# One product in four of a selective scan goes from VectorE to GpSimd, with a new order of all engines' steps

## Chip, cores and metric

One core of a Trainium2 chip runs the whole program in one launch. The metric is the device time of an execution in microseconds. All data is fp32.

## Reference

The input x is 8 sequences (batches) of 512 tokens of 128 values. Six layers follow each other, each added to its input:

```python
x = x + 0.5 * ffn0(layernorm(x))        # norm, 128->512, gelu, norm, 512->128, ternary weights
x = x + attn0(layernorm(x))             # small scan over the tokens, 16 states
x = x + 0.5 * ffn0(layernorm(x))
x = x + 0.5 * ffn1(layernorm(x))        # encoder, router over 8 experts, top 2, decoder, norm
x = x + attn1(layernorm(x))             # selective scan, below
x = x + 0.5 * ffn1(layernorm(x))
```

attn1 has 256 inner channels d with 16 states n each. After a projection and a convolution over 3 tokens give u and a gate, and a projection of u gives B, C and (with a softplus) delta, it computes in chunks of 32 tokens, each starting from zero:

```python
dA  = exp(delta[l, d] * A[d, n])
dBu = delta[l, d] * B[l, n] * u[l, d]
h   = dA * h + dBu                      # along the tokens of a chunk
y[l, d] = sum over n of h * C[l, n]
out = (y * silu(res)) @ W_out + b_out
```

## The kernel before

A batch is one tile of 512 tokens. Its work is cut into parts, and every engine has four threads of parts: F (the two ffn0 layers and attn0), P (everything that uses the one PSUM bank pp: the router half of ffn1, called front, twice per batch; the part of attn1 ahead of the scan; and the product with W_out behind it), E (the experts and the decoder of ffn1, called back) and S (the selective scan). The parts of pp take turns in a fixed row (P_TURNS), and a turn starts when the one before has left the bank (bank_free). Several batches are under way at once: while one is in its scan, a later one is in ffn0.

Inside an engine the order of all steps is written out by hand: ORDER has one string per engine, one letter per step, and side_by_side takes the next step of the thread that the letter names. An engine issues in that order and waits at a step until its semaphores are there. A further letter K in TensorE's string is a filler: a product of a tile of zeros (256 columns) that adds nothing to yp. There are 44 of them in 33 places.

The scan of a batch has 16 steps (2 channel halves c of 128 by 8 pairs of states k), 128 steps in all, and each step j has two half-steps r, one per state, of 128 x 512 elements:

- SyncE loads the rows of B and C, broadcast to 128 partitions, into b_row and c_row (three slots each; L502, L509). A slot is free when its last reader is done.
- GpSimd makes dbu of a whole step, du times b_row (L708, 128 x 1024); dbu has two buffers, so it waits for the scans of step j - 2. du itself (L635) needs delta, the last output of the part ahead of the scan.
- ScalarE makes dA of a half-step, the exponential (L1207), into one of two PSUM banks. It waits until the product of the half-step before in that bank is done, since that reads the bank.
- VectorE runs the scan in place in that bank (L982) and then the product with C into hs (L989), which has two buffers.
- TensorE adds the product into yp through the identity (L1483), in the order of the steps. At the end of each channel half VectorE multiplies yp with the gate (yg, L997).

TensorE's products take two passes in fp32, so a step of 512 columns is two instructions in the profile. The other lines that matter here: L1228 with pp and yg (the product with W_out), L1151 (delta), L662 and L675 (GpSimd's multiplication by the norm's gain and its addition in the back part), L1300 (a product of attn0), L1492 (the filler).

Of the kernel before, what the change touches and what calls it, by code (L numbers as in the profile page):

```python
# [27 lines left out]
ALU = mybir.AluOpType  # L28
# [33 lines left out]
    "PE":
        "PFEPFEFFFFFFFFFFFFFFFFFFFFFFFFPFPFFPFFPFPEFFPPPKKKKEKFEFEEEFEFEKKFFKFPFPFFFPFFPPPKPFPFKKFFSSKPSFSFPS"
        "FPSFPSSFKPESSSPSKSKSFSFSESEFSEFEESESFSESFFSFSSSSFFFSPFFPSSSPFSPFPFPFPFFPFFFSKKSPSSPSPSPSEPSFSFPSPSSF"
        "SSFESKESEFSFEESSFESSFSESFFSFSFFSSPSPPFSSPFSPFFPFPKFFPFFSSPSSPSSPSPSEPSFSFPSPSPKSSFEPSEPFEPSEPEPESFEF"
        "SEFFSEFSFEFPSEFPEEPESSPSESSPSFSPSSPSKPFSFSFFSKFPSFPSFPSFKPSSFSEPSSSPKKKPSPSFPSFEPSSEPSEFEEPFEPEFFESF"
# [1524 lines left out]
```

## Time and profile before

| | us |
|---|---|
| median of 3 runs | 1121.41 |
| fastest and slowest of them | 1113.58 and 1122.65 |
| span of the profiled execution, first to last instruction | 1116.6 |
| the profiled execution's own time | not listed apart from the runs |
| TensorE busy (modelled ends) | 935.0 |
| VectorE busy | 762.5 |
| ScalarE busy | 659.4 |
| GpSimd busy | 515.7 |
| mean granted clock of TensorE, of full speed | 0.933 |

The profile is one execution. Busy times overlap between engines; the matmuls are pipelined and their ends are modelled, so TensorE's share is no measure of how near it is to its peak. An engine's idle time costs something only where a later step waits for it.

### The profile page before, as it was taken

Reading aid. Unit: us, or ns where it says so; the run is one execution under the profiler, and the core shown is the slowest. Engines: PE = TensorE matmul, PEld = TensorE weight load, DVE = VectorE, ACT = ScalarE, POOL = GpSimd, SP = SyncE. Lnnn points to the kernel's source line nnn. Section 1 sums busy time; section 2 is a strip of 40 time slices with the busy share of each in tenths; the row PEclk is TensorE's granted clock in tenths of the full one; section 3 lists DMA queues with packets and bytes.
Section 4 is the critical chain, followed back from the end, with each engine's and each line's share of the span. In section 5 each row is a group of like instructions: output and inputs, shape, how many; then the busy total and the mean of one; then the engine's idle time right before and its main releaser. Section 6 shows DMA issues by size and latency. Waiting matters only on the chain.

```text
span 1116.6 us, 11275 instructions
## 1 busy us (share of the span) xinstructions
PE 935.0 (84%) x3446; PEld 451.9 (40%) x3446; DVE 762.5 (68%) x1717; ACT 659.4 (59%) x1030; POOL 515.7 (46%) x413
## 2 busy tenths in 40 slices
PE   6457888799889979998999799969996898689865
PEld 4234344344434434444444344434433343343332
DVE  3213417983898388878896699748974959499921
ACT  4344557576657765796668855866585424644221
POOL 2131227462745365556454654555454616555311
PEclk9668999999989989999999999989998899889986
DMA  3002017441735263456252744255434525374320
GB/s 136 10 1 86 1 54 249 143 132 48 246 120 164 73 229 130 167 158 210 86 181 96 227 180 163 92 172 208 142 123 136 202 108 206 119 270 134 142 86 9
DMA packets 44717, 151.83 MB, mean 136 GB/s; under 512 B 4464, under 2 KB 12784, under 8 KB 40560
## 3 DMA queue, kind: packets, MB, share of 16 engines
q1 hardware_dynamic: 44656, 151.11, 39.5%
q8 instruction: 27, 0.44, 0.2%
q14 instruction: 34, 0.28, 0.1%
HBM read 148.21 MB, written 2.88 MB: 135 GB/s over the span
## 4 chain that ended last, share of the span: by engine, by line
PE 46%; DVE 25%; ACT 14%; issue 6%; POOL 6%; DMA 2%; SPq 0%; DVEq 0%; POOLq 0%; ACTq 0%
DVE dA L982 11%; PE yp L1483 9%; ACT L116 5%; PE mp L1442 5%; PE pp L1362 4%; PE mp L1427 3%; PE fp L1264 3%; PE fp L1248 3%; PE pp L1228 3%; DVE hs L989 3%; ACT dA L1207 2%; PE mp L1451 2%; POOL dbu L708 2%; PE mp L1228 2%; PE pp L1332 1%
## 5 line engine op out<-in xcount | busy, mean ns | idle before, releaser
L708 POOL TENSOR_TENSOR dbu<-du,b_row 128x1024 f32<-128x1024 f32 x128 | 301.2, 2356 | 178.8 <-DVE dA L982 176.9
L982 DVE TENSOR_TENSOR_SCAN dA<-dA,dbu 128x512 f32<-128x512 f32 x256 | 312.4, 1220 | 75.5 <-ACT dA L1207 41.5
L1483 PE MATMUL yp<-hs,ident 128*128 128x512 f32 x512 | 273.1, 636 | 58.2 <-DVE hs L989 57.7
L1207 ACT ACTIVATE dA<-delta,pr 128x512 f32<-128x512 f32 x256 | 173.8, 686 | 104.3 <-DVE hs L989 103.1
L989 DVE TENSOR_TENSOR hs<-dA,c_row 128x512 f32<-128x512 f32 x256 | 177.0, 691 | 28.1 <-PE yp L1483 18.2
L116 ACT ACT_TABLE_LOAD x130 | 166.8, 1283 | 15.0 <-POOL delta L639 11.4
L1483 PEld LDWEIGHTS yp<-hs,ident 128*128 128x128 f32 x512 | 89.7, 196 | 169.4 <-DVE hs L989 101.7
L1427 PE MATMUL mp<-cont,ex_ 64*128 64x512 f32 x128 | 75.5, 671 | 15.5 <-DVE he L940 11.6
L1431 PE MATMUL mp<-cont,ex_ 64*128 64x512 f32 x128 | 75.6, 672 | 3.2 <-DVE he L945 3.2
L1248 PE MATMUL fp<-sq,w 128*128 128x512 f32 x128 | 71.1, 679 | 5.7 <-ACT sq L1030 4.1
L1264 PEld LDWEIGHTS fp<-w,hT 128*128 128x128 f32 x512 | 63.5, 193 | 29.2 <-issue 14.1
L1264 PE MATMUL fp<-w,hT 128*128 128x129 f32 x512 | 66.6, 279 | 5.4 <-ACT sq L1030 2.1
L940 DVE SCALAR_TENSOR_TENSOR he<-mp,nb_e,gsp 128x512 f32<-128x512 f32 x64 | 47.5, 742 | 23.7 <-PE mp L1427 15.9
L1442 PE MATMUL mp<-he,ex_ 128*64 128x512 f32 x128 | 63.6, 640 | 0.0
L1444 PE MATMUL mp<-he,ex_ 128*64 128x512 f32 x128 | 63.6, 640 | 0.0
L662 POOL TENSOR_TENSOR dg<-eoT,ex_ 128x512 f32<-128x512 f32 x16 | 17.5, 1092 | 78.6 <-DVE eoT L949 78.6
L805 DVE COPY fs<-fp 128x4 f32<-128x4 f32 x16 | 2.5, 157 | 70.9 <-PE fp L1284 70.9
L1362 PE MATMUL pp<-p_zT,mw_cv 128*128 128x512 f32 x96 | 48.9, 618 | 0.8 <-ACT du L1137 0.8
L1043 ACT ACTIVATE hT<-fp,b 128x512 f32<-128x512 f32 x64 | 42.6, 685 | 11.3 <-PE fp L1248 10.6
L569 POOL TENSOR_SCALAR f_vv<-f_mv 128x4 f32<-128x4 f32 x24 | 4.6, 193 | 94.0 <-DVE f_mv L774 93.5
L945 DVE SCALAR_TENSOR_TENSOR he<-mp,nb_e,gsp 128x512 f32<-128x512 f32 x64 | 47.5, 742 | 0.0
L1178 ACT ACTIVATE eoT<-mp 128x512 f32<-128x512 f32 x16 | 9.5, 596 | 58.3 <-PE mp L1444 58.3
(219 smaller groups left out, 1426.9 us busy)
## 6 DMA issues: line engine op xcount, KB each, us to landing
b_row<-held SPq DMA_DIRECT2D x104, 512.0 KB, 4.9
c_row<-held SPq DMA_DIRECT2D x104, 512.0 KB, 4.1
gsp<-gheld SPq DMA_DIRECT2D x32, 1024.0 KB, 6.6
xin<-L_attn_x SPq DMA_DIRECT2D x8, 256.0 KB, 3.0
out<-xb SPq DMA_DIRECT2D x8, 256.0 KB, 2.3
ex_<-c_ex SPq DMA_DIRECT2D x1, 1001.0 KB, 8.0
b_row<-c_ps SPq DMA_DIRECT2D x1, 768.0 KB, 9.4
pr<-c_pr SPq DMA_DIRECT2D x1, 567.0 KB, 10.4
```

Source lines behind the costliest of these rows:

```text
L116: self.act.preload_act_table_set(sets[0])
L708: pool.tensor_tensor(out=dbu[:, j % 2, :].rearrange("p (r t) -> p r t", r=2), in0=d, in1=b_n, op=ALU.mult).then_inc(dbu_r.sem, 1)
L982: dve.tensor_tensor_scan(out=dA[:, half], data0=dA[:, half], data1=dbu[:, j % 2, half], initial=0.0, op0=ALU.mult, op1=ALU.add).then_inc(h ...
L989: dve.tensor_tensor(out=hs[:, j % 2, half], in0=dA[:, half], in1=c_row[:, C_ROWS.slot[j], half], op=ALU.mult).then_inc(hc_r.sem, 1)
L1207: act.activation(out=dA[:, r * SEQ:(r + 1) * SEQ], in_=delta[:, i % 2, c, :], func=ACT.Exp, scale=mA[:, c, 2 * k + r:2 * k + r + 1]).then_ ...
L1248: pe.matmul(fps[(c + 1) % 2], lhsT=w1[:, c * P:(c + 1) * P], rhs=fzT, start=True, stop=True).then_inc(h_ps.sem, 1)
L1264: pe.matmul(o[:, q, 0:P + 1], lhsT=hT[:, c, q * P:(q + 1) * P], rhs=w2[:, c, 0:P + 1], start=(c == 0), stop=(c == HC - 1))
L1362: last = pe.matmul(pp[:, :], lhsT=mw_cv[:, k, c * P:(c + 1) * P], rhs=pzT[:, k:k + SEQ], start=(k == 0), stop=(k == TAPS - 1))
L1427: pe.matmul(mps[0], lhsT=w_e1[0:MOE, k, :], rhs=cont[0:MOE, m % 2, :], start=True, stop=True).then_inc(hee_ps.sem, 1)
L1431: pe.matmul(mps[1], lhsT=w_e1[MOE:2 * MOE, k, :], rhs=cont[MOE:2 * MOE, m % 2, :], start=True, stop=True).then_inc(heo_ps.sem, 1)
L1442: last_e = pe.matmul(mps[0][0:MOE, :], lhsT=w_e2[:, 2 * k, :], rhs=he[:, 2 * k, :], start=False, stop=(k == EP - 1))
L1483: pe.matmul(yp[:, :], lhsT=ident[:, :], rhs=hs[:, j % 2, r * SEQ:(r + 1) * SEQ], start=(s % PAIRS == 0 and r == 0), stop=(s % PAIRS == PAI ...
```

## The change

Of the 128 scan steps, those with j % 4 == 1 (32 steps, 64 half-steps, four steps per batch) get their product with C on GpSimd. For them VectorE's scan writes its result into hs in SBUF instead of into the PSUM bank, after it has waited for the sum that last read this buffer; GpSimd multiplies hs in place by c_row, in a new thread C; TensorE's sum and SyncE's next load of that slot wait for GpSimd's semaphore instead of VectorE's; ScalarE's next exponential in the bank waits for the scan only. The other 96 steps work as before. All five order strings are new: GpSimd's has 64 letters C more, TensorE's no K; the counts of all other letters are the same. The fillers, their tile of zeros and its memset are gone. ScalarE loads its table before it waits for the start of a scan instead of after, and GpSimd's product L662 waits for its own addition of the back part before.

```diff
-    "Pool":
-        "PFEFFFFFFFFFPFPFPFFFEEFEPPFFPSSPFSPSSSSFSFSFSSFSFSSEESEPPSFFFPSSPSPFSSFSFSSSSFSSSFEESESPFFSPFSPSSFPSP"
...
+    "Pool":
+        "FPFFFEFFFFFFPFFFFFPPFEEEPPFFFPPSSSCSCFSSFSCCSSFSFFSSCECSPEEPSSFSCCPFFPPSSSCCFSSFPSSCCSSFFSEESCEPFSCS"
...
-FILL = 256
...
+POOL_STEPS = 4
+
+
+def on_pool(j):
+    return j % POOL_STEPS == 1
+
+
+class Products:
+
+
+    def __init__(self, by_vector, by_pool):
+        self.by_vector, self.by_pool = by_vector, by_pool
+
+    def wait(self, eng, h):
+        j, r = divmod(h, 2)
+        some = sum(on_pool(x) == on_pool(j) for x in range(j))
+        eng.wait_ge(self.by_pool if on_pool(j) else self.by_vector, 2 * some + r + 1)
...
-        zeros = sb("zeros", [P, P])
...
-        hc_r = signal("hc_r", STEPS)
+        hc_v, hc_p = sem("hc_v"), sem("hc_p")
+        products = Products(hc_v, hc_p)
...
                             if C_ROWS.after[j] >= 0:
-                                sp.wait_ge(hc_r.sem, 2 * (C_ROWS.after[j] + 1))
+                                products.wait(sp, 2 * C_ROWS.after[j] + 1)
...
                 pool.wait_ge(ddr.sem, ddr.at(m, 1))
+                if m >= 1:
+                    stage, i = M_TURNS[m - 1]
+                    added = hx_new if stage == "moef" else xo_new
+                    pool.wait_ge(added.sem, added.at(i, 1))
...
+            def c_thread():
+                for j in range(BATCH * STEPS):
+                    if not on_pool(j):
+                        continue
+                    for r in range(2):
+                        half = slice(r * SEQ, (r + 1) * SEQ)
+                        yield True
+                        pool.wait_ge(hs_r.sem, 2 * j + r + 1)
+                        if r == 0:
+                            pool.wait_ge(c_in[C_ROWS.slot[j]], 16 * C_ROWS.load[j])
+                        pool.tensor_tensor(out=hs[:, j % 2, half], in0=hs[:, j % 2, half],
+                                           in1=c_row[:, C_ROWS.slot[j], half], op=ALU.mult).then_inc(hc_p, 1)
...
+                            if on_pool(j):
+                                if j >= 2:
+                                    dve.wait_ge(sum_ps.sem, h - 3)
+                                dve.tensor_tensor_scan(out=hs[:, j % 2, half], data0=dA[:, half],
+                                                       data1=dbu[:, j % 2, half], initial=0.0, op0=ALU.mult,
+                                                       op1=ALU.add).then_inc(hs_r.sem, 1)
+                                continue
...
+                            table(ACT.Exp)
                             if h % (2 * STEPS) == 0:
                                 act.wait_ge(start_r.sem, start_r.at(i, 1))
-                            table(ACT.Exp)
-                            if h >= 2:
-                                act.wait_ge(hc_r.sem, h - 1)
+                            if h >= 2 and on_pool(j - 1):
+                                act.wait_ge(hs_r.sem, h - 1)
+                            elif h >= 2:
+                                products.wait(act, h - 2)
...
-                            pe.wait_ge(hc_r.sem, 2 * j + r + 1)
+                            products.wait(pe, 2 * j + r)
...
-            def k_thread():
...
-            side_by_side(ORDER["PE"], F=f_thread(), P=p_thread(), E=e_thread(), S=s_thread(), K=k_thread())
+            side_by_side(ORDER["PE"], F=f_thread(), P=p_thread(), E=e_thread(), S=s_thread())
```

Counted letter by letter, the steps shift against each other. On TensorE, the last matmul of the part ahead of the scan of batch i stands behind this many of the 32 half-steps of the scan before it, for i = 1 to 7: before 31, 31, 30, 31, 32, 32, 32; in the change 31, 27, 27, 26, 28, 26, 26. The product with W_out of batch i = 0 to 6 stands behind this many half-steps of the next scan: before 10, 15, 16, 15, 14, 16, 10; in the change 7, 9, 10, 10, 10, 11, 10. In GpSimd's list the C steps of step j mostly stand behind the dbu of step j + 1, in some places behind that of step j + 2 too. ScalarE's table changes, counted along its list, are 130 before and 127 in the change.

## Rows read from the trace of the kernel before

**Rows 1.** The page: busy time and share by engine; VectorE in 40 slices.

```profile
PE 935.0 (84%) x3446; PEld 451.9 (40%) x3446; DVE 762.5 (68%) x1717; ACT 659.4 (59%) x1030; POOL 515.7 (46%) x413
...
DVE  3213417983898388878896699748974959499921
```

**Rows 2.** The page: the chain that ended last, by engine.

```profile
PE 46%; DVE 25%; ACT 14%; issue 6%; POOL 6%; DMA 2%; SPq 0%; DVEq 0%; POOLq 0%; ACTq 0%
```

**Rows 3.** Windows: length, busy PE, PEld, DVE, ACT, POOL, clock, DMA share, GB/s.

```profile
180.00:200.00 20.00, 18.93 (x83) 9.79 (x82) 19.03 (x43) 11.19 (x18) 10.68 (x7) 1.00 0.50 170
...
720.00:740.00 20.00, 15.45 (x70) 8.26 (x69) 8.35 (x28) 11.78 (x18) 6.01 (x7) 0.96 0.32 83
...
1040.00:1060.00 20.00, 17.43 (x55) 6.89 (x55) 18.58 (x29) 3.05 (x5) 5.67 (x3) 1.00 0.27 109
```

**Rows 4.** Groups by line: count, busy us, mean ns, idle before, releasers.

```profile
L982 DVE TENSOR_TENSOR_SCAN dA<-dA,dbu 128x512 f32<-128x512 f32 x256 | 312.4, 1220 | 75.5 <-ACT dA L1207 41.5 <-POOL dbu L708 33.4
...
L708 POOL TENSOR_TENSOR dbu<-du,b_row 128x1024 f32<-128x1024 f32 x128 | 301.2, 2356 | 178.8 <-DVE dA L982 176.9 <-DMA b_row<-held 1.9
...
L989 DVE TENSOR_TENSOR hs<-dA,c_row 128x512 f32<-128x512 f32 x256 | 177.0, 691 | 28.1 <-PE yp L1483 18.2 <-issue 1.3
...
L1492 PE MATMUL yp<-w,zeros 128*128 128x256 f32 x88 | 30.4, 456 | 5.0 <-DVE m_top L924 5.0
...
L662 POOL TENSOR_TENSOR dg<-eoT,ex_ 128x512 f32<-128x512 f32 x16 | 17.5, 1092 | 78.6 <-DVE eoT L949 78.6
...
L675 POOL TENSOR_TENSOR hx<-xf,dg 128x512 f32<-128x512 f32 x8 | 10.1, 1267 | 5.5 <-ACT dg L1025 5.5
```

**Rows 5.** The same windows, products of line 989 alone: length, VectorE, clock.

```profile
180.00:200.00 20.00, 5.53 (x8) 1.00 0.50 170
...
1040.00:1060.00 20.00, 4.15 (x6) 1.00 0.27 109
...
sum 900.00, DVE 176.99; mean DVE 3.93
```

**Rows 6.** Timeline, joints between scans: start, length, engine, line, idle before.

```profile
282.70 1.23 DVE L982 TENSOR_TENSOR_SCAN dA<-dA,dbu 128x512 f32<-128x512 f32 x1 [0.68 <-POOL dbu L708]
...
387.39 2.35 POOL L635 TENSOR_TENSOR du<-delta,du 128x1024 f32<-128x1024 f32 x1 [18.27 <-ACT delta L1151]
...
392.41 1.23 DVE L982 TENSOR_TENSOR_SCAN dA<-dA,dbu 128x512 f32<-128x512 f32 x1 [0.89 <-POOL dbu L708]
...
497.68 1.22 DVE L982 TENSOR_TENSOR_SCAN dA<-dA,dbu 128x512 f32<-128x512 f32 x1
...
503.77 1.23 DVE L982 TENSOR_TENSOR_SCAN dA<-dA,dbu 128x512 f32<-128x512 f32 x1 [1.37 <-POOL dbu L708]
```

**Rows 7.** Timeline, the middle of the scan of batch 3.

```profile
545.41 1.22 DVE L982 TENSOR_TENSOR_SCAN dA<-dA,dbu 128x512 f32<-128x512 f32 x1
...
560.03 1.95 PE L1228 MATMUL pp<-pr,yg 128*128 128x128 f32 x16
...
563.34 1.23 DVE L982 TENSOR_TENSOR_SCAN dA<-dA,dbu 128x512 f32<-128x512 f32 x1
```

**Rows 8.** Waits: who waited for whom; total us, times, longest.

```profile
PEld yp L1483 <- DVE hs L989: 101.7, 88, 8.6
...
DVE dA L982 <- POOL dbu L708: 33.4, 10, 10.9
```

**Rows 9.** The chain at 106.90 us, then the timeline of line 1300.

```profile
106.90 3.59 PE yp L1492 x8
...
40.85 2.07 PE L1300 MATMUL fp<-sq,at 128*128 128x512 f32 x2 [0.69 <-ACT sq L1030]
...
540.58 1.02 PE L1300 MATMUL fp<-sq,at 128*128 128x512 f32 x2
```

**Rows 10.** Windows at 40 and 620 us, columns as in rows 3.

```profile
40.00:60.00 20.00, 8.05 (x25) 4.52 (x24) 4.45 (x15) 8.64 (x13) 2.82 (x4) 0.59 0.00 0
620.00:640.00 20.00, 16.28 (x50) 8.19 (x51) 12.21 (x13) 18.55 (x26) 14.15 (x10) 0.91 0.69 231
```

More of the change, by code:

```diff
@@ L47 @@
+        "FSSFSCFPCPPSSSPCCSPFSFSPSCFCSFSEFESESPCSCPFSSSCFCSPPFSEESCCSPPFSSFFSSPCESCFSSEEEPCSSSCFFSFSCCSPPPSFS"
+        "PSCCSEEPFSPFSEFSCCSFSSEEEFSPSCCFSSSPCFSCPPSESEFPSECPSCFSFFPSCSCSFFSEEESPCSSCPSSFSCCSPPSSCPSCSPESESCC"
+        "ESPSSSEEESPCCSSPSSSCCPPSSSCCSEESSSCCSSPESSCCPSSEEPSSECSCPEPEEEEE",
     "DVE":
-        "FEFFPEFFFFFFFFFFPPPFFPFEEEEEEEEFFFEPFFFPSSSSSSSSSSSPPFSFSFSSSEESSEESEFEESFEFSSSSSESSSPSSSFSFFPSSFSSS"
-        "SSFSFSSSPPSSSPSSFSEEFSEEFEESSESSESSSSESSSPSFSFFPSSSSSFSSSSSSFSFSSPPPSSSSEESEEFEESEFPPEFSPSSESEESPEES"
@@ L62 @@
[L62 to L70 removed]
+        "FFFPFFEFFFFFFFFPEPFPFFPEEEEFEEFEFEEPFFFPFSSSSSSSPPFSFSSSSSEESEEEEEESFSFFSSSSSSESSSPSSFSSFPFSSSSSSSSS"
@@ new lines @@
+        "FSSPPFSFSSSSSEESEEEESESEFSFFSSESPSPSSSSFSFSPSFSSSSSSSSSSSPPPSFSFSFSSEPEPSEESEEFPESSFEFSSSESSESPESSSS"
+        "FSEEFFSPEEESSSSSESSSESSSSSPPPFSSFFSSEESSEEPEEPESSEFSFSFSSESPSESPESSSSSFESEFSSFEESESSESPSSESSSSSPPPSF"
+        "SFSFSEESPPEESESEFSEEFFSSSSPESSSEPESEESSSFSEESSFSESEFSSSPSSESSSSPPPSSSFSSFEEFSEEPPEEESSFSEFSFSSESPSSP"
+        "EESESSSSSESEESFSSESESSFPSSSSSSSEPPPSSSSSSSEESEEPEEPEESSSSPESSSSPEEPSSSSEESSESEESESSSSSSSSSSSESSPPSSS"
+        "SSSSEEEESEESEESSSPSSPSSESSSSSPPSSSSSSEEPPEEEEEEPPEEEEEEEEEE",
@@ new lines @@
+    "PE":
+        "PFFFFFFFFFFFFFFEFFFFFFFFFFFPFPFPFFPFEFPFPFFEPPFFEFEFEEEFEFEFFFFPFFFPPPFPFPFPFPFPFFFFPPSSPPSPSPSESSSS"
+        "FFSSSEFESEESFESSEFESFSFSSFSFFSSFFFPSSSPSSPSPSPSPFPFPSFFPFPFFPSFFPSPESSSSPSPSSFSFSESESEFSEEFSESEFFFFF"
+        "FSSSFPFFSPSSPSPSPSSPFPSFPSSFFSSPFFPSFPPFPFESSPSSSPPSPSPFPSFSPEFEPESFSEESEFSEFSFSSFEFFFSSEFFPSPSPSSEP"
+        "SEPESPSSPESPSESFSSEFPFPFPSPFFFPFFPSESSPPSPSSPFSEFPSESFESPEPFESSESESSFSFEFFFSFSFESPFPFPSPSSSEPSSPESFP"
+        "EPESESSSSFEPFPFSPFFFPPSSFFPSSSEPPSPPFEPSSFPSESPFSEFEESESSSFEFSFEFSFSFEFEPFPFSSPSSSPSESPEPESSPSPEFSES"
+        "SPFSPFFPPSPSFFPFEFFSSPSPSSPSPEPFEFSEPESFFEPESSEFSFSFSFSFEFFSEPFPSSPFPSSESPSSPSESPEPSESSESPSSPEPPSPSS"
+        "PSESSPSPSPSPEPSSEEPEEPSESSESSSESEPSPSSPESSSPEPSEPEPSPESSSSSSEPSPSPSPSPPSSSSSSPESSESESSESEEESSEPPSSPS"
+        "PSSPSSPESSSSSSSPEEPPEPEPEPEPEEEEEEEEE",
@@ L557, in _ @@
             ch.add(pool.memset(by32[:, :], 1.0 / 32))
-            ch.add(pool.memset(zeros[:, :], 0.0))
             ch.add(pool.memset(pzT[:, 0:TAPS - 1], 0.0))
@@ L989, in s_thread @@
                             dve.tensor_tensor(out=hs[:, j % 2, half], in0=dA[:, half],
-                                              in1=c_row[:, C_ROWS.slot[j], half], op=ALU.mult).then_inc(hc_r.sem, 1)
+                                              in1=c_row[:, C_ROWS.slot[j], half], op=ALU.mult).then_inc(hc_v, 1)
                         if s % PAIRS == PAIRS - 1:
@@ L1485, in s_thread @@
                                       ).then_inc(sum_ps.sem, 1)
-            def k_thread():
-                order = ORDER["PE"]
-                for at in (n for n, name in enumerate(order) if name == "K"):
-                    yield True
-                    alone = order[:at].count("S") in (0, 2 * BATCH * STEPS)
-                    pe.matmul(yp[:, 0:FILL], lhsT=zeros[:, :], rhs=w1[:, 0:FILL], start=alone, stop=alone,
-                              skip_group_check=True)
-            side_by_side(ORDER["PE"], F=f_thread(), P=p_thread(), E=e_thread(), S=s_thread(), K=k_thread())
+            side_by_side(ORDER["PE"], F=f_thread(), P=p_thread(), E=e_thread(), S=s_thread())
 def stacked(*parts):
```

33 lines of the change are left out of this document (11 added, 22 removed).

## The prediction

> **What bounds the kernel now.** I read five views in this order. First the page's busy times and slices [rows 1]: no engine is full over the span (TensorE 84%, VectorE 68%), but VectorE's row swings between 9 and 1. That is the thing to see: it is full in some stretches and starved in others, so its mean says little. Second, the chain that ended last [rows 2]: it passes from engine to engine, 46% of the span on TensorE, 25% on VectorE, 6% on GpSimd. Third, windows of 20 us over the stretch with scans, 160 to 1060 us [rows 3]: in 21 of 45 windows VectorE is busy 17.5 us or more (first and last shown, with 720 as one of the others: 8.35). So VectorE ends the wait in about half of the stretch only.
>
> Fourth, the joints between two scans [rows 6]. Before batch 2, du waited 18.27 us for delta, that is for the before-scan part, and the first scan follows at 392.41. From the last scan of batch 2 to the first of batch 3 it takes 6.1 us (497.68 to 503.77). Fifth, the middle of a scan [rows 7]: from 545.41 to 563.34 no scan starts, since yg (L997) stands behind the product with W_out of the batch before (560.03) which has its turn in bank pp only then. These two waits come from the serial turns of pp, not from VectorE's load.
>
> **The base of the sum.** The profiled execution has a span of 1116.6 us; its own time is not listed apart. The median of the three runs, 1121.41, lies 4.8 above that span, the fastest run 3.0 below. I sum against the span and add 4.8 at the end. About 1% (11 us) is what a measurement of this kernel can tell from no change.
>
> **VectorE's products.** 32 of 128 steps give up two products of 0.691 us [rows 4]: 64 x 0.691 = 44.2 us of busy time. On the path they lie only where VectorE is full. The 21 full windows hold 91.2 of the 177.0 us of products (in [rows 5] the first, the last and the sum), 51.5%, so 0.515 x 44.2 = **-22.8 us** (bounds 0 and -44.2). The other half falls where VectorE waits anyway. No row has a scan into SBUF. The nearest are the scan into PSUM, 1.220 us, and the product, which reads PSUM, writes SBUF and goes faster [rows 4]; I keep 1.22, and a tenth of a microsecond each way on 64 scans would be 6 us. ScalarE may start the next exponential after the scan instead of after the product, 0.69 us earlier, but VectorE's next scan is all that this feeds, so it is in the 22.8 already.
>
> **GpSimd's products.** Half of L708's 2.356 us is 1.18; other 128x512 products take 1.092 (L662) to 1.267 (L675) [rows 4]. I take 1.18, nearest in its operands: 64 x 1.18 = 75.5 us of GpSimd's time (70 to 81), from 515.7 to 591 us of busy time. It isn't full after that, so what counts is who stands behind. On GpSimd the next dbu does: for step j+2 it may start only when scan j is done, and the second product now comes first. 1.18 + 2.36 = 3.54 us, and VectorE reaches scan j+2 after two scans and two products, 2 x 1.22 + 2 x 0.69 = 3.8 us. The cover is 0.3 us, gone whenever one of GpSimd's other products (1.09 to 1.27 us) slips between. All 32 exposed would be 32 x 1.18 = 38 us. Until now scans waited for dbu 10 times in 128, 33.4 us in sum [rows 8], while dbu waited 176.9 us for scans [rows 4]; I take about a fifth, **+8**.
>
> On TensorE every later instruction stands behind the sum of a GpSimd step. With GpSimd free, the second product is ready 1.18 - 0.69 = 0.49 us later than from VectorE, 16 us over 32 steps; with one dbu queued ahead it is 2.36 + 0.49 = 2.85, 91 us. TensorE's weight loads already wait for a product 88 times, 101.7 us in sum, at 256 sums [rows 8]; the new list puts the sums of these steps further back, and the chain is on TensorE for less than half of its length: **+3**, ends -10 (other matmuls go first) and +42 (0.46 x 91).
>
> The rows of C for these steps come free later, and so do all loads queued behind them on SyncE. With three slots a row is asked for some three steps ahead, 3 x 3.8 = 11 us; a product that is late by 2.85 us eats a quarter of that. Nothing added; without that cover the price is that of the slow rival below.
>
> The Trainium skill, in "GPSIMD Engine Reference", 4.1 Engine selection, speaks against the move: for elementwise work it says VectorE and not GpSimd, about twice as slow with two inputs (3.1: 1.96 times). By that page a product would be an estimated 1.96 x 0.691 = 1.35 us; the halved row of this trace gives 1.7 times. By the page the two GpSimd terms would grow by some 2 us.
>
> **Filler products.** 44 of them (88 passes, 30.4 us busy [rows 4]) in 33 places go. Most are in places where TensorE waits; one group of 3.59 us stands on the chain at 106.90 us [rows 9], so -4. Against it: the granted clock. At 180 to 200 us, with TensorE busy 18.93 us of 20, it is 1.00 [rows 3]; at 40 to 60 us, busy 8.05, it is 0.59 [rows 10], a mix of the levels 2.4 and 1.2 GHz. At the lower one the pair of passes L1300 takes 2.07 instead of 1.02 us [rows 9]. Where the fillers stood, some stretches will now be granted at half. I take +5, net **+1**; ends -30 and +27 (rival below).
>
> **The new order.** Counted letter by letter, the before-scan part of batch i (i = 1 to 7) is moved forward on TensorE: its last matmul stood behind 30 to 32 of the 32 half-steps of the scan before it; now behind 26 to 28, but for batch 1 (31 as before). The product with W_out of batch i comes 7 to 11 half-steps into the next scan instead of 10 to 16. Both aim at the waits in [rows 6, 7]. If every joint fell to the 6.1 us of the best, the seven (23.6, 21.4, 6.1, 7.9, 19.8, 17.3 and 12.8, all read like the third) would give back 66 us. But the period doesn't follow the joint: the batch that ends in the joint of 6.1 us takes 111.4 us from first scan to first scan (392.41 to 503.77), the one that ends in 21.4 takes 109.7 (282.70 to 392.41) [rows 6]. A short joint was paid by a longer scan. I take **-9**, ends -66 and +10 (what is moved forward holds up other work: half of one stall like [rows 7]). ScalarE's table loads fall from 130 to 127 by the letters, and one moves ahead of the wait for start_r, where the first dbu (2.36 us) covers it: both zero. The wait before dg is for an addition that GpSimd issued long before; the memset of zeros is at the start: zero.
>
> **Sum.** -22.8 + 8 + 3 + 1 - 9 = -19.8; 1116.6 - 19.8 + 4.8 = 1101.6 us.
>
> **Rivals.** *The bank pp sets the period.* Its turns (two routers, one before-scan, one product with W_out per batch) form a serial row, and [rows 7] shows VectorE's work waiting for it. For: joints and middles stall at VectorE idle. Then the relief stays only in the first and the last scan, which have no such neighbours in full: about 2 x 8 halves x 0.69 = 11 us, eaten by 8 + 3: 1121.
>
> *TensorE stuck behind GpSimd.* The sums come in order of step, and GpSimd has the dbu of a later step in front of the product in several places of its list. Price 2.85 us per step, 32 steps, times 0.46 of the chain: +42. Then 1121.4 - 22.8 + 42 + 8 + 1 - 9 = 1141. It decides from the point where some 17 of the 32 steps have a whole dbu ahead (17 x 2.85 x 0.46 = 22.3, which eats the gain). Against it: GpSimd idled 178.8 us before L708 [rows 4].
>
> *The clock.* Each of the 33 places loses what 620 to 640 us lost (0.91 instead of 1.00 over 20 us [rows 10], so 1.8 us of work): 59 us, times 0.46: +27 instead of +5: 1124. The Trainium skill, "TensorE: Matmul & The Clock Gate", Why this matters for your kernels, asks to leave no idle gaps between bursts, or the clock falls back. The trace agrees at 40 to 60 us; by that rule the change would end here.
>
> *The joints close.* If two thirds of the 66 us come back: 1101.6 + 9 - 44 = 1067. *The change isn't what it says:* the lists hold 64 letters C and no K, so I give it no chance.
>
> **How the numbers follow.** Forecast 0.48 (its own range 1084 to 1110), joints close 0.10, pp sets the period 0.16, clock 0.09, stuck behind GpSimd 0.17. Faster by over 1%: 0.48 + 0.10 = 0.58; within 1%: 0.25; slower: 0.17. The range 1072 to 1136 leaves out most of the closing joints and the worse half of the slow rival, under 2 in 10.
>
> **What would show it.** VectorE's busy time near 718 us with 192 products; GpSimd near 591; scans into hs still 1.22 us; GpSimd's product 1.09 to 1.27. Right: fewer windows with VectorE over 17.5 us, scans waiting for dbu under some 45 us. Wrong: TensorE's waits before the sums naming GpSimd's product with more than 40 us; the mean granted clock well under the 0.933 of the span now; or joints under 8 us throughout, with a time near 1070.

## The result, and the profile after

The changed kernel takes 1062.81 us (median of 4 runs, 1058.22 to 1066.8) against 1121.22: a ratio of 0.9489 [0.9442, 0.9535], 58 us less. Forecast were 1101.6 us, 20 less, with a range down to 1072. So the side was right, and the forecast size less than half of what came: the time lies at the rival "the joints close" (1067). The profiled execution took 1066.8 us at a span of 1064.9; its mean granted clock is 0.932 (0.933 before).

From the page of the changed kernel: busy time by engine, VectorE's slices, the chain by engine, and the groups that answer to [rows 1, 2, 4].

```profile
PE 918.2 (86%) x3358; PEld 436.9 (41%) x3358; DVE 732.6 (69%) x1653; ACT 651.6 (61%) x1027; POOL 593.8 (56%) x476
...
DVE  3223322996298839885988789777978988699731
...
PE 58%; DVE 17%; ACT 14%; issue 6%; POOL 5%; DMA 0%; DVEq 0%; SPq 0%; POOLq 0%; ACTq 0%
...
L730 POOL TENSOR_TENSOR dbu<-du,b_row 128x1024 f32<-128x1024 f32 x128 | 301.4, 2359 | 112.1 <-DVE dA L1024 90.7
...
L1024 DVE TENSOR_TENSOR_SCAN dA<-dA,dbu 128x512 f32<-128x512 f32 x192 | 234.1, 1219 | 58.3 <-ACT dA L1251 48.9
...
L1031 DVE TENSOR_TENSOR hs<-dA,c_row 128x512 f32<-128x512 f32 x192 | 132.7, 691 | 17.0 <-PE yp L1527 10.4
L743 POOL TENSOR_TENSOR hs<-hs,c_row 128x512 f32<-128x512 f32 x64 | 80.8, 1271 | 41.0 <-DVE hs L1020 40.7
...
L1020 DVE TENSOR_TENSOR_SCAN hs<-dA,dbu 128x512 f32<-128x512 f32 x64 | 76.0, 1209 | 5.4 <-ACT dA L1251 4.7
```

The prices came as forecast: GpSimd's product 1.271 us (taken at 1.18, bounds 1.09 to 1.27), the scan into SBUF 1.209 (taken at 1.22), GpSimd 593.8 us busy (591). VectorE is busy 732.6 us, where 718 were forecast; the last experiments show what the other 14 are. What wasn't forecast is the chain: 12 points have moved onto TensorE, and VectorE's share fell from 25% to 17%. Between the first and the last scan VectorE's row had six slices of 3, 4 or 5 [rows 1]; now there are three of 5 or less, a 2, a 3 and a 5, at the first three joints.

The waits of the changed kernel (total us, times, longest), beside [rows 8]:

```profile
POOL du L653 <- ACT delta L1193: 43.1, 8, 16.4
...
PEld yp L1527 <- DVE hs L1031: 28.8, 34, 3.7
...
PEld yp L1527 <- POOL hs L743: 9.3, 12, 2.0
...
DVE dA L1024 <- POOL dbu L730: 8.9, 3, 5.5
```

TensorE's weight loads wait 28.8 + 9.3 us for products where they waited 101.7; scans wait for dbu 8.9 us where it was 33.4. So neither of the two costs that the prediction put on GpSimd's products shows as a growing wait. Three joints of the changed kernel, on VectorE's timeline (start, length, engine, line, idle before), beside [rows 6]: the last scan of a batch and the first of the next.

```profile
272.88 1.23 DVE L1024 TENSOR_TENSOR_SCAN dA<-dA,dbu 128x512 f32<-128x512 f32 x1 [6.71 <-ACT dA L1251]
...
284.89 1.23 DVE L1024 TENSOR_TENSOR_SCAN dA<-dA,dbu 128x512 f32<-128x512 f32 x1 [5.47 <-POOL dbu L730]
...
387.43 1.23 DVE L1024 TENSOR_TENSOR_SCAN dA<-dA,dbu 128x512 f32<-128x512 f32 x1 [8.13 <-ACT dA L1251]
...
395.06 1.22 DVE L1024 TENSOR_TENSOR_SCAN dA<-dA,dbu 128x512 f32<-128x512 f32 x1
...
821.73 1.22 DVE L1024 TENSOR_TENSOR_SCAN dA<-dA,dbu 128x512 f32<-128x512 f32 x1
...
826.44 1.22 DVE L1024 TENSOR_TENSOR_SCAN dA<-dA,dbu 128x512 f32<-128x512 f32 x1
```

12.0, 7.6 and 4.7 us. GpSimd's du of the next batch starts ahead of the second of them, by 4.5 us:

```profile
382.89 2.34 POOL L653 TENSOR_TENSOR du<-delta,du 128x1024 f32<-128x1024 f32 x1 [6.05 <-ACT delta L1193]
```

In the kernel before, du starts behind the last scan at every joint (18.6, 16.4, 1.1, 2.9, 14.6, 12.4 and 7.8 us), and the first scan follows 5.0 to 5.2 us after it: that is the joint. In the changed kernel du is late at the first joint only (5.5 us) and starts 2.7 to 4.8 us ahead of the last scan at the other six. The sum of du's waits for delta says nothing of this: 45.6 us before, 43.1 now.

A scan can also pause at its middle, between the two channel halves, where VectorE's list has the addition behind the product with W_out ahead of yg and of the next scan: [rows 7] in batch 3, and this in batch 6 of the kernel before, 21.6 us from one start to the next:

```profile
895.92 1.22 DVE L982 TENSOR_TENSOR_SCAN dA<-dA,dbu 128x512 f32<-128x512 f32 x1
...
916.34 0.69 DVE L885 TENSOR_TENSOR xb<-pp,hx 128x512 f32<-128x512 f32 x1 [7.72 <-PE pp L1228]
...
917.54 1.22 DVE L982 TENSOR_TENSOR_SCAN dA<-dA,dbu 128x512 f32<-128x512 f32 x1
```

Reading all seven joints, the eight scans (first to last start) and their middles (start of the 16th scan of a half-step to the 17th) of each profiled kernel in this way gives the table on which the experiments rest; tail is the time from the start of the last scan to the end of the span:

| kernel | first scan at | scans, sum of 8 | of these the middles | joints | sum | tail | span |
|---|---|---|---|---|---|---|---|
| before | 169.7 | 772.9 | 73.0 | 23.6 21.4 6.1 7.9 19.7 17.4 12.8 | 109.0 | 64.9 | 1116.6 |
| e3: before, no fillers | 171.4 | 777.9 | 77.3 | 23.7 21.1 6.1 7.9 19.7 18.1 12.8 | 109.5 | 65.5 | 1124.3 |
| e1: new lists, VectorE's products | 179.8 | 776.6 | 47.9 | 12.0 7.6 10.7 9.8 6.9 4.7 4.2 | 56.0 | 68.8 | 1081.2 |
| changed | 179.8 | 760.8 | 48.8 | 12.0 7.6 10.8 9.8 6.9 4.7 4.2 | 56.1 | 68.0 | 1064.9 |

From before to changed the span loses 51.7 us: 10.1 are added ahead of the first scan and 3.1 in the tail, 12.1 are saved in the scans and 52.9 in the joints.

### The profile page after: what moved, and what is told of

Same layout as the page of the kernel before. It is cut to its first block, busy times and chain, and to the rows that moved or that the text cites. A ratio compares the mean times of both kernels' runs of the same rounds, so it can differ in the third digit from the quotient of the medians.

```text
span 1064.9 us, 11114 instructions
## 1 busy us (share of the span) xinstructions
PE 918.2 (86%) x3358; PEld 436.9 (41%) x3358; DVE 732.6 (69%) x1653; ACT 651.6 (61%) x1027; POOL 593.8 (56%) x476
## 4 chain that ended last, share of the span: by engine, by line
PE 58%; DVE 17%; ACT 14%; issue 6%; POOL 5%; DMA 0%; DVEq 0%; SPq 0%; POOLq 0%; ACTq 0%
PE yp L1527 14%; PE mp L1486 5%; DVE dA L1024 5%; PE mp L1471 5%; ACT L117 4%; PE pp L1406 4%; PE pp L1272 4%; PE fp L1308 4%; PE fp L1292 4%; PE mp L1272 2%; PE pp L1376 2%; PE mp L1495 2%; PE mp L1480 1%; DVE hs L1020 1%; ACT hT L1085 1%
## 5 line engine op out<-in xcount | busy, mean ns | idle before, releaser
L1527 PE MATMUL yp<-hs,ident 128*128 128x512 f32 x512 | 264.1, 625 | 11.9 <-DVE hs L1031 9.3
L1024 DVE TENSOR_TENSOR_SCAN dA<-dA,dbu 128x512 f32<-128x512 f32 x192 | 234.1, 1219 | 58.3 <-ACT dA L1251 48.9
L1031 DVE TENSOR_TENSOR hs<-dA,c_row 128x512 f32<-128x512 f32 x192 | 132.7, 691 | 17.0 <-PE yp L1527 10.4
L743 POOL TENSOR_TENSOR hs<-hs,c_row 128x512 f32<-128x512 f32 x64 | 80.8, 1271 | 41.0 <-DVE hs L1020 40.7
L1471 PE MATMUL mp<-cont,ex_ 64*128 64x512 f32 x128 | 80.2, 709 | 7.5 <-DVE he L975 6.6
L1308 PEld LDWEIGHTS fp<-w,hT 128*128 128x128 f32 x512 | 66.9, 205 | 36.6 <-ACT hT L1085 14.9
L1308 PE MATMUL fp<-w,hT 128*128 128x129 f32 x512 | 72.2, 295 | 11.1 <-ACT hT L1085 6.0
L1475 PE MATMUL mp<-cont,ex_ 64*128 64x512 f32 x128 | 81.0, 716 | 0.0
L1020 DVE TENSOR_TENSOR_SCAN hs<-dA,dbu 128x512 f32<-128x512 f32 x64 | 76.0, 1209 | 5.4 <-ACT dA L1251 4.7
L1292 PE MATMUL fp<-sq,w 128*128 128x512 f32 x128 | 68.3, 650 | 5.5 <-ACT hT L1085 3.4
L1486 PE MATMUL mp<-he,ex_ 128*64 128x512 f32 x128 | 66.1, 651 | 0.0
L1488 PE MATMUL mp<-he,ex_ 128*64 128x512 f32 x128 | 66.1, 650 | 0.0
L684 POOL TENSOR_TENSOR dg<-eoT,ex_ 128x512 f32<-128x512 f32 x16 | 17.5, 1094 | 60.7 <-DVE eoT L984 60.7
L1406 PE MATMUL pp<-p_zT,mw_cv 128*128 128x512 f32 x96 | 49.7, 627 | 1.5 <-ACT du L1179 0.8
```

The lines of the kernel that those rows point to most:

```text
L1020: dve.tensor_tensor_scan(out=hs[:, j % 2, half], data0=dA[:, half], data1=dbu[:, j % 2, half], initial=0.0, op0=ALU.mult, op1=ALU.add).the ...
L1024: dve.tensor_tensor_scan(out=dA[:, half], data0=dA[:, half], data1=dbu[:, j % 2, half], initial=0.0, op0=ALU.mult, op1=ALU.add).then_inc(h ...
L1031: dve.tensor_tensor(out=hs[:, j % 2, half], in0=dA[:, half], in1=c_row[:, C_ROWS.slot[j], half], op=ALU.mult).then_inc(hc_v, 1)
L1292: pe.matmul(fps[(c + 1) % 2], lhsT=w1[:, c * P:(c + 1) * P], rhs=fzT, start=True, stop=True).then_inc(h_ps.sem, 1)
L1308: pe.matmul(o[:, q, 0:P + 1], lhsT=hT[:, c, q * P:(q + 1) * P], rhs=w2[:, c, 0:P + 1], start=(c == 0), stop=(c == HC - 1))
L1406: last = pe.matmul(pp[:, :], lhsT=mw_cv[:, k, c * P:(c + 1) * P], rhs=pzT[:, k:k + SEQ], start=(k == 0), stop=(k == TAPS - 1))
```

## The experiments

Two theories stood at the start. **The order:** the new lists alone close the joints, and the prediction under-priced that one term. **The products:** it is VectorE's relief that lets the joints close, so that the lists alone give little. A ratio is to the kernel before, run on the same chip; one hundredth is some 11 us.

**e1, the new lists with all products on VectorE.**

```diff
 def on_pool(j):
-    return j % POOL_STEPS == 1
+    return False
```

The 64 letters C are struck from GpSimd's list, which is otherwise as in the changed kernel.

Expected: 

> The new order lists with all products back on VectorE (GpSimd's 64 letters C struck out, every scan in PSUM as before, no fillers). Theory A, VectorE's relief is the gain: most of the 58 us are lost, 1100 us or more. Theory B, the order alone closes the joints and the relief is worth what the prediction priced (about 23 us less 11): 1060 to 1078, with joints summing to 55 to 70 us. Theory C, the order needs the relief, since the pp turns that it moves forward stand in VectorE's queue among products: between 1080 and 1115, with scans longer by 4 to 6 us each and the joints partly open again.

Measured: 1082.78 us, 0.9683 [0.9648, 0.9718]. Its joints (table) are those of the changed kernel to a tenth of a microsecond. The lists close them; the products have no part in it. The time lies 5 us over the range of theory B. The middle of batch 3 in e1, 5.3 us where [rows 7] has 17.9:

```profile
559.17 1.22 DVE L1023 TENSOR_TENSOR_SCAN dA<-dA,dbu 128x512 f32<-128x512 f32 x1
...
564.50 1.22 DVE L1023 TENSOR_TENSOR_SCAN dA<-dA,dbu 128x512 f32<-128x512 f32 x1
```

**e3, the kernel before without its 44 fillers**: the letters K struck from TensorE's list, whose first line is shown.

```diff
-        "PFEPFEFFFFFFFFFFFFFFFFFFFFFFFFPFPFFPFFPFPEFFPPPKKKKEKFEFEEEFEFEKKFFKFPFPFFFPFFPPPKPFPFKKFFSSKPSFSFPS"
+        "PFEPFEFFFFFFFFFFFFFFFFFFFFFFFFPFPFFPFFPFPEFFPPPEFEFEEEFEFEFFFPFPFFFPFFPPPPFPFFFSSPSFSFPSFPSFPSSFPESS"
```

Expected: 

> The kernel before with the 44 fillers struck out and nothing else. The prediction's term: +1 us, so 1119 to 1125, with a mean granted clock of 0.92 to 0.93. Rival, the fillers hold the clock up: 1135 or more, clock under 0.915. Rival, the fillers only stand in the way: 1105 to 1115.

Measured: 1127.01 us, 1.0085 [1.0052, 1.0117], mean granted clock 0.905 instead of 0.933: the clock of the first rival, at a time between its range and the forecast's. With e1 the whole change now splits in three: fillers out +0.0085, new order -0.0402 (1.0085 to 0.9683), products to GpSimd -0.0194 (to 0.9489); in microseconds of 1121 about +9.5, -45 and -22. In the spans the order is -43.1: joints -53.5, scans -1.3, first scan +8.4, tail +3.3.

The -1.3 is the difference of two large numbers. The middles lose 29.4 us, nearly all in batches 3 (18.5 to 5.3) and 6 (23.3 to 7.4); the rest of the scans grows by 28.2, of which 15.9 in batch 1, 11.9 in batch 6 and 5.1 in batch 0. So joints and middles together give back 82.9 us, and about a third of that returns as longer scans.

e1 also keeps two small parts of the change that aren't lists, ScalarE's earlier table load and the wait before L662; no run takes them apart. The traces leave them little: in the kernel before, du, the dbu behind it and a short copy between them take 4.95 of the 5.0 to 5.2 us from du to the first scan, and the idle time before the multiplication by the gain is put down to VectorE's eoT alone, before [rows 4] and after (60.7 us).

**e2, the old lists with GpSimd's products**, no fillers; the letters C stand behind the dbu of step j+1, or of j+2 where the old lists would otherwise wait in a ring (about half). The first line of GpSimd's list:

```diff
-        "PFEFFFFFFFFFPFPFPFFFEEFEPPFFPSSPFSPSSSSFSFSFSSFSFSSEESEPPSFFFPSSPSPFSSFSFSSSSFSSSFEESESPFFSPFPSSPFSP"
+        "PFEFFFFFFFFFPFPFPFFFEEFEPPFFPSSPFSPSCCSSSFCCSFSFSSFCCSFSSEESEPCCPSFFFPSSPSPFSCCSFSFSCSCSSFSSCCSFEESE"
```

Expected: 

> The old order lists, fillers struck out, with one product in four on GpSimd: each pair of letters C stands behind the dbu of step j+1 or, where the old lists would lock up otherwise, of step j+2. Theory A: VectorE loses 44 us of work, the time falls by 15 to 30 us, to about 1095 to 1106. Theory B: joints stay near the 109 us of before, 1112 to 1125. Theory C: no gain, 1115 to 1135, since the old lists hold TensorE and VectorE behind a product that comes later.

Measured: 1227.67 us, 1.0979 [1.094, 1.1019], 100 us more than e3, outside what any theory gave. Its waits:

```profile
POOL dbu L730 <- DVE dA L1024: 164.6, 43, 22.8
PEld yp L1527 <- POOL hs L743: 121.7, 43, 7.6
```

TensorE's weight loads wait 121.7 us for GpSimd's products (changed kernel: 9.3); the matmuls' own waits for them lie inside these. That is the prediction's rival "TensorE stuck behind GpSimd": 100 / 32 = 3.1 us for each step, where it had 2.85 for a step and 0.46 of it on the path. The rival was real, and it is the lists that decide whether it comes.

**e4, the changed kernel with the before-scan part put back**: on four engines the letters of this part, for batches 2 to 7, stand again no earlier than behind the scan half-step at which the old lists had them. A line of GpSimd's list:

```diff
-        "PSCCSEEPFSPFSEFSCCSFSSEEEFSPSCCFSSSPCFSCPPSESEFPSECPSCFSFFPSCSCSFFSEEESPCSSCPSSFSCCSPPSSCPSCSPESESCC"
+        "PSCCSEEPFSPFSEFSCCSFSSEEEFSSPCCFSSSPCFSCPPSESEFPSECPSCFSFFPSCSCSFFSEEESCSSCSPSPFSCCSPPSSCPSCSPESESCC"
```

Expected: 

> The changed kernel with only the part ahead of the scan of batches 2 to 7 put back, on TensorE, ScalarE, VectorE and GpSimd, to where the old lists had it against the half-steps of the scan (TensorE's last matmul of it behind 30 to 32 half-steps instead of 26 to 28); products on GpSimd, no fillers. Theory A: VectorE's load is the same, within 8 us of the changed kernel (1055 to 1071). Theories B and C: the joints open again, from 56 us in sum to 90 or more, and the time goes to 1085 to 1110.

Measured: 1179.49 us, 1.0547 [1.0508, 1.0585]. Joints 12.0, 28.5, 17.4, 18.3, 24.3, 19.8, 15.8, sum 136.0, and du waits for delta three times as long as in the changed kernel:

```profile
POOL du L653 <- ACT delta L1193: 128.0, 8, 28.0
```

At the joints ahead of these six batches du starts 3.9 to 13.8 us behind the last scan again, while the middles stay short (49.7 us in sum). So the place of this part opens and closes the joints, as the first theory has it. The loss of 117 us lies far outside every range and is more than the order's whole gain: old places among new neighbours are worse than the old lists were.

**e10, the reverse in the old lists** (no fillers): the letters of the before-scan part go forward by 1 to 3 half-steps, as far as the other lists allow, and those of the after-scan part not at all. The last line of GpSimd's list:

```diff
-        "EFFPSPFSSPSSSPFSPSFSFSSFSEEFESPSPSSEEEFPSPSSSSSPSPSSPSSEEESPPSSSSEEEPSPSPSSSSSSPSPSSSSEESESSPPEEEEEE",
+        "EFPFSPFSSPSSSPFSPSFSFSSFSEEFESPPSSSEEEFPSPSSSSSPSPSSPSSEEESPPSSSSEEEPSPSPSSSSSSPSPSSSSEESESSPPEEEEEE",
```

Expected: 

> The kernel before without fillers (1127.0 us), its old lists, and only the steps of the before-scan and after-scan parts put forward on all engines as far as the lists of the others allow without a lock: 1 to 3 half-steps for the before-scan parts, none for the products with W_out. If the joints were open because the input of these parts comes late from the other threads, nothing closes: joints 105 to 112 us, 1118 to 1130. Rival, the mere place of the part's instructions behind the last scans holds it: each half-step forward gives 2 to 3 us in each joint, joints 85 to 100, 1105 to 1118.

Measured: 1141.55 us, 1.0203 [1.0148, 1.0258]. The joints sum to 106.4: nothing closes, and it is slower than e3, with the scans of batches 0 and 4 longer by 5.0 and 12.7 us. Why these two grew wasn't followed. The change moves the part by 3 to 6 half-steps in six of the seven batches, and moves what feeds it as well; so far the part alone can't go in the old lists.

**e6, each of GpSimd's products done twice.** The first of the two also waits for GpSimd's own earlier instructions of its chain (ch).

```diff
+        spare = sb("spare", [P, SEQ])
...
+                        ch.wait()
+                        ch.add(pool.tensor_tensor(out=spare[:, :], in0=hs[:, j % 2, half],
+                                                  in1=c_row[:, C_ROWS.slot[j], half], op=ALU.mult))
                         pool.tensor_tensor(out=hs[:, j % 2, half], in0=hs[:, j % 2, half],
```

Expected: 

> The changed kernel with each of GpSimd's 64 products done twice, the first time into a spare tile: 64 x 1.27 = 81 us more on GpSimd, nothing else moved. If the prediction's two terms for what stands behind such a product (the next dbu, TensorE's sums) are right in kind, with a cover of only 0.3 us, a product that takes twice as long is paid nearly in full: +38 us when one of the two per step is exposed, +81 when both are, so 1100 to 1144. Rival: the new lists leave room behind GpSimd's products (dbu waits for dA of ScalarE in most steps anyway), and less than a quarter of the 81 us is seen: 1063 to 1083.

Measured: 1100.7 us, 0.9793 [0.9768, 0.9817], 34 us more. GpSimd's busy time grows by 77.3 us (671.1), so 0.44 of each added microsecond is paid and 0.56 is covered: the lower edge of what was expected. By the profiles 26.4 of the 35.8 us by which the scans grow lie in batches 0, 1 and 7; the five between have room behind these products. The chain shows where they stand (5% on GpSimd without the doubling):

```profile
PE 42%; DVE 18%; POOL 16%; ACT 13%; issue 9%; DMA 2%; SPq 0%; DVEq 0%; POOLq 0%; ACTq 0%
```

**e5 and e9, half of the products**: steps 1 and 9 of each batch (e5), or 5 and 13 (e9); the other letters C are struck.

```diff
-POOL_STEPS = 4
+POOL_STEPS = 8
```

In e9 the remainder is another one too:

```diff
-    return j % POOL_STEPS == 1
+    return j % POOL_STEPS == 5
```

Expected of e5: 

> The changed kernel with the products of every eighth step on GpSimd instead of every fourth: 32 of the 64 products are VectorE's again, the lists are the changed kernel's but for the 32 letters struck. In proportion: all 64 products were worth 20.0 us (1082.8 to 1062.8), so 32 are worth 10 and this kernel takes 1069 to 1076, its scan phases summing to 765 to 772 us. Rival, the relief saturates because VectorE's first free microseconds are the ones on the path: 1062 to 1067. Rival, GpSimd's products carry a cost of their own (the dbu behind them) that VectorE's relief only just outweighs, so half the relief brings half the cost and nothing is seen of it until the last: 1077 to 1083. The joints stay at 56 us in all of them, since the lists set them.

Expected of e9: 

> The changed kernel with GpSimd's products in steps 5 and 13 of each batch only (the run with every eighth step had them in steps 1 and 9). From scan to scan, in the profiles, the changed kernel is shorter than its lists with all products on VectorE by 6.6 us over the 16 steps of numbers 1 and 9, by 18.4 us over those of 5 and 13, and longer by 9.4 us over all other steps; the first half alone kept the 6.7 and had none of the 18.4. If a product's worth is that of its place: 18 us shorter in steps 5 and 13, nothing in 1 and 9, 4 to 9 us given back elsewhere, so 9 to 14 us under 1082.8: 1069 to 1074, a ratio of 0.957 to 0.962. Rival, the number of products counts and not the place: as the first half, a ratio of 0.963 to 0.968, 1076 to 1084. Rival, the products of steps 1 and 9 only cost: 1058 to 1064.

Measured: e5 1084.05 us, 0.9653 [0.9625, 0.9682]; e9 1064.96 us, 0.9522 [0.9458, 0.9585]. With none it is 0.9683, with all 0.9489. Not the number counts but the place: steps 5 and 13 bring 0.016 of the 0.019 (more than was expected of them), and e5 can't be told from the kernel with none. From scan to scan, against e1, the changed kernel's steps 5 and 13 are shorter by 18.4 us in sum (e9: 18.6), its steps 1 and 9 by 6.6, and all other steps, which keep VectorE's products, are longer by 9.4 (e9: 3.9). So the products of steps 1 and 9 give little, and something gets longer elsewhere. By step, step 9 gives 5.5 us and step 1 only 1.1.

**What takes it back in step 1.** Step 1 of batch 6 in the changed kernel: first GpSimd's timeline, then VectorE's for three operations of the router (start, length, engine, line).

```profile
833.74 2.35 POOL L730 TENSOR_TENSOR dbu<-du,b_row 128x1024 f32<-128x1024 f32 x1
836.04 1.26 POOL L743 TENSOR_TENSOR hs<-hs,c_row 128x512 f32<-128x512 f32 x1
837.26 2.34 POOL L730 TENSOR_TENSOR dbu<-du,b_row 128x1024 f32<-128x1024 f32 x1
```

```profile
835.06 1.05 DVE L895 COPY two<-m 128x8 f32<-128x8 f32 x1
...
836.84 0.52 DVE L903 SCALAR_TENSOR_TENSOR mr<-mr,ex 128x32 f32<-128x32 f32 x1
...
837.82 1.83 DVE L910 TENSOR_TENSOR g<-mr,sm 128x32 f32<-128x32 f32 x1
```

Operations on 8 or 32 columns last up to 1.83 us, and each ends with the GpSimd instruction beside it: 836.11 against 836.09, 837.36 against 837.30, 839.65 against 839.60. Each is done 16 times; the groups of the changed kernel:

```profile
L895 DVE COPY two<-m 128x8 f32<-128x8 f32 x16 | 11.7, 730 | 0.0
...
L910 DVE TENSOR_TENSOR g<-mr,sm 128x32 f32<-128x32 f32 x16 | 9.2, 574 | 0.6
...
L903 DVE SCALAR_TENSOR_TENSOR mr<-mr,ex 128x32 f32<-128x32 f32 x16 | 7.6, 473 | 1.8 <-ACT ex L1156 1.5
```

28.5 us in sum; 27.6 in e5, but 17.1 in e9, 16.7 in e1 and 13.5 in the kernel before: the growth from 13.5 accounts for the 14 us of VectorE that weren't forecast. What goes beyond 0.18 us each lies in step 1 with 10.2 us in the changed kernel and in e5, with 2.5 in e1 and e9, and in step 9 with none. So it is GpSimd's product of step 1 that meets the router. Whether it also costs the time is what the last three runs test.

**e12, e13, e14, the router's mask in PSUM**: in the changed kernel, in e5, and in e7 (below).

```diff
-        mr = sb("mr", [P, TILES, EXPERTS])
...
                 lg = pp[:, 32:64].rearrange("p (q e) -> p q e", q=TILES)
+                mr = pp[:, 64:96].rearrange("p (q e) -> p q e", q=TILES)
```

Expected of e12: 

> The changed kernel with the router's mask mr in 32 columns of bank pp instead of SBUF, so that L903 and L910 read one input from PSUM. In the changed kernel these two take 7.6 and 9.2 us on 16 calls each, 0.19 us where no GpSimd instruction runs beside them and up to 1.84 where one does. If the stretch comes from two inputs in SBUF beside GpSimd: every call at 0.2 to 0.3 us, some 10 us of VectorE's time back, of which half on the path: ratio 0.941 to 0.946 (0.9489 without). Rival, the stretch has another cause: the calls keep up to 1.8 us and the time stays. Rival, the stretch goes but lies where VectorE waits anyway: the time within 0.3% of 0.9489.

Expected of e13: 

> The kernel with products of steps 1 and 9 on GpSimd (ratio 0.9653) and the mask in PSUM. If the stretched router operations took back what these products gave: 0.957 to 0.961. Rival, the products stand where they give nothing in any case: within 0.3% of 0.9653.

Expected of e14: 

> The kernel with 69 fillers (0.9366) and the mask in PSUM. If both gains add: 0.929 to 0.934, the fastest so far. Rival, nothing on top: 0.935 to 0.940.

Measured: e12 1048.23 us, 0.9366 [0.9325, 0.9406]; e13 1070.79, 0.9577 [0.9542, 0.9612]; e14 1037.16, 0.929 [0.9245, 0.9334]. The groups of e12:

```profile
L903 DVE SCALAR_TENSOR_TENSOR pp<-pp,ex 128x32 f32<-128x32 f32 x16 | 3.2, 198 | 1.6 <-ACT ex L1156 1.3
L910 DVE TENSOR_TENSOR g<-pp,sm 128x32 f32<-128x32 f32 x16 | 3.1, 191 | 0.6
```

16.8 us became 6.3, none of the two is stretched any more, and the three kernels gain 0.012 (more than was expected), 0.008 and 0.008. The copy (L895) still reads SBUF alone and still takes 12.3 us. From scan to scan, step 1 of e12 is 8.6 us shorter than in e1, where it was 1.1: 7.5 us, as much as its stretch has shrunk (10.2 to 2.3). The steps that keep VectorE's products are longer by 4.5 in sum instead of 9.4. In e1 the two operations take 8.4 us, 2.1 over the 6.3, so the mask in PSUM has little to win there; that kernel wasn't run.

**e7 and e8, fillers in the new lists**: 69 matmuls on zeros ahead of steps before which TensorE stood still, or the first 27 of them alone. Counted by the sums around them, 28 stand before the first scan, 35 in the scans and 6 in the tail (the expectation has 27, 38 and 4). They are issued as in the kernel before; the first line of TensorE's list:

```diff
-        "PFFFFFFFFFFFFFFEFFFFFFFFFFFPFPFPFFPFEFPFPFFEPPFFEFEFEEEFEFEFFFFPFFFPPPFPFPFPFPFPFFFFPPSSPPSPSPSESSSS"
+        "PFFFFFFFFFFFFFFEFFFFFFFFFFFPKKKKKKKKKKKKKKFPFPFFPFEFPFPFFEPPKKKKKKKKKKKFFEFEKFEEEFEFEFFFFPKFFFPPPFPF"
```

Expected of e7: 

> The changed kernel with 69 filler matmuls put into TensorE's list ahead of steps before which TensorE stood still in the changed kernel's trace: 27 before the first scan, 38 in the scans, 4 in the tail. The 44 of the kernel before were worth 9.6 us there (1127.0 without, 1117.4 with them) with a granted clock of 0.933 against 0.905. If the clock still has something to give: granted clock over 0.945, time 1050 to 1058. Rival: the new lists keep TensorE at work and the clock at 0.932 by themselves, so the fillers do nothing that can be measured: 1060 to 1066. Rival: some of them stand ahead of work that would have been ready, and 69 x 0.22 us of matmul add up to 1066 to 1078.

Expected of e8: 

> The run above with only the 27 fillers that stand before the first scan. TensorE's clock in the first 180 us is where the kernel before had most of its fillers' effect by the prediction (4 us earlier start). If so: first scan 3 to 5 us earlier than 179.84 and the time 1058 to 1060. Rival: the start waits for loads and ScalarE and not for the clock: first scan within 1 us, time 1062 to 1064. What the run above has beyond this one belongs to the fillers inside the scans and the tail.

Measured: e7 1051.18 us, 0.9366 [0.9336, 0.9396], mean granted clock 0.962; e8 1061.28, 0.9438 [0.9407, 0.9468], clock 0.943, not told apart from the changed kernel's 0.9489. In e8's profile the first scan comes at 174.5 us, 5.3 earlier than in the changed kernel, and nothing else moves; but e7, with the same fillers and one more ahead of it, starts its first scan at 178.8, so what they give at the start isn't settled. (The expectation has the prediction's 4 us the other way round: there the fillers delayed the start.) The windows of 100 us from 100 and from 900 (length, busy PE, PEld, DVE, ACT, POOL, clock, DMA share, GB/s), first of the changed kernel, then of e7:

```profile
100.00:200.00 100.00, 75.19 (x265) 35.94 (x266) 41.17 (x135) 52.81 (x83) 37.18 (x35) 0.85 0.27 92
...
900.00:1000.00 100.00, 87.57 (x262) 36.54 (x260) 86.20 (x148) 52.24 (x85) 68.98 (x45) 0.95 0.59 199
```

```profile
100.00:200.00 100.00, 82.03 (x313) 41.20 (x312) 44.06 (x143) 53.77 (x85) 38.12 (x38) 0.93 0.27 94
...
900.00:1000.00 100.00, 88.25 (x298) 39.79 (x296) 86.37 (x157) 47.19 (x82) 67.34 (x45) 1.00 0.54 185
```

Between 400 and 800 us the clock is 0.97 to 1.00 in either kernel. The scans of e7 sum to 754.2 us instead of 760.8: the gain lies where the clock had fallen, in batches 0, 6 and 7 and in the tail (65.2 instead of 68.0).

**e11, steps 5 and 13 alone with the fillers of e7.**

Expected: 

> Steps 5 and 13 on GpSimd and the 69 fillers of the run with fillers throughout. That run's ratio was 0.9366 with all 64 products on GpSimd. If the fillers' gain (0.012 in the ratio) adds to the half's: 0.945 to 0.950. Rival, the shorter stay behind GpSimd pays once TensorE's clock is up: under 0.935, faster than every kernel so far.

Measured: 1054.11 us, 0.9419 [0.9352, 0.9485]: between the two ranges, and not told apart from e7. The version to keep is e14, faster than both kernels.

## Why the prediction was wrong

**The new order is the step that failed.** The prediction had -9, of an end at -66; e3 to e1 is about -45 (0.0402). These 36 us are nearly all of the 39 by which the forecast missed. Two things were wrong in this term. First, it argued that "the period doesn't follow the joint", from two batches of the kernel before, one with a short joint and a long scan, its neighbour the other way round, and took 57 of the 66 us as paid back. The runs show less: joints lose 53.5 us and middles 29.4, and the rest of the scans grows by 28.2, about a third. Batch 1, the one with the short scan, does pay 15.9 of it, so the observation was sound and the rule drawn from it wasn't. Second, the middles had no price: the prediction read one of them [rows 7], named it as an aim of the new lists, and summed joints alone. What the order cost, 8.4 us ahead of the first scan and 3.3 in the tail, wasn't counted either. Whether the scans grow because the joints close or because of other new places in the lists, no run separates.

**The products' relief** was -22.8; the 32 steps are shorter by 25.0 (18.4 + 6.6) in the profile. Right in size, though the mean over full windows hid that most of it (18.4) lies in half of the steps. In e12, with the router out of the way, it is 33.5 (19.4 + 14.1).

**What stands behind GpSimd** was +8 and +3; the other steps are longer by 9.4 us. The size is near, by luck, and the cause is another. The waits that it named fell. The router's operations on VectorE, which it didn't look at, took 11.8 us more than in e1; e12 and e13 show that this costs time, in step 1 above all, and that about half of the 9.4 hangs on it. What the other half is wasn't followed. That a longer product is paid for (cover 0.3 us) was right in kind, and too dear: e6 pays 0.44 of it. The products' net was forecast at -11.8, and is -15.8 in the scans of the profile and some -22 (0.0194) in the timed runs.

**The fillers** were +1 and are +9.5 in the old lists (e3). The clock's price was taken too low, and no start was won: without them the first scan comes 1.7 us later, where -4 was taken. In the new lists the clock is back at 0.932 without one filler; e7 shows that there was still something to win, 0.012.

**The rivals.** The bank pp doesn't set the period: with the same number of its turns e1 takes 43 us less than e3. The clock's +27 didn't come. "Stuck behind GpSimd" came in e2 at more than its price and is avoided by the new lists. "The joints close" was the right one, at a chance of 0.10. Its 44 us for the order are what came, though with the middles in them; that its 1067 is so near rests also on luck, since the fillers cost 8.5 us more and the products gave some 10 more than it had. Its sign, joints under 8 us throughout, didn't come: three of the seven are 9.8 to 12.0.

**Left open:** how much of the order's gain is the before-scan part's place and how much what feeds it (e4 shows that the new lists need the place; e10 could move it too little to test the reverse), which letters shortened the middles, why the rest of the scans grew, and why steps 1 and 9 give less than 5 and 13 even with the mask in PSUM.

## What to carry to other kernels

When an order of steps is to close idle stretches, list all of them, inside the phases as well as between them, and price each; here two pauses in the middle of scans were worth half as much as seven joints. How much comes back as longer work elsewhere is for an experiment: two batches said nearly all, the runs a third. Relief on an engine is worth what the steps give in which it is taken, so put it where that engine ends the wait, and look at what the taking engine runs beside. Before work goes to GpSimd, look for small VectorE operations that read SBUF alone and will run beside it: one input in PSUM freed them here, for 32 columns of a bank.

## What the hardware showed

L895, L903 and L910 run 48 times in the changed kernel, 29 times starting while a GpSimd instruction runs. 27 of these end 0.03 to 0.05 us after that instruction; one has only 0.07 us of it left and takes its usual 0.16 us, and one runs through in 0.19 us beside an operation on 4 columns. The other 19 take 0.16 to 0.19 us. The length depends on what is left of the GpSimd instruction, 1.92 us at most, and not on the columns. The scans and the products with one input in PSUM keep their 1.22 and 0.691 us beside the same work. The Trainium skill, "SBUF — State Buffer", Who interferes with whom, states this: a VectorE instruction with two inputs in SBUF and a GpSimd instruction that reads SBUF, or a VectorE copy in a two-port mode and any GpSimd instruction, exclude each other, and the later one waits to the end. The trace agrees in these 27; that the copy runs in such a mode no run here shows. e12 shows the price of L903 and L910, 0.012 of the time.

GpSimd's product takes 1.271 us, 1.84 times VectorE's 0.691 (the Trainium skill, "GPSIMD Engine Reference", 3.1 Elementwise — side-by-side cycle accounting, has 1.96 for a longer addition), and moving it still pays 0.019: the ratio of the two engines told nothing of the path.
